# Mamba-2 layer and FFN on one core: decay blocks of 64 tokens instead of 128, with the order of the engines' work rewritten around them

## The chip, the cores and the metric

One core of one Trainium2 chip. The metric is device time in microseconds of one launch, as the median of 3 runs. Engines are called as in the profile: PE (TensorE matmul), PEld (its weight loads), DVE (VectorE), ACT (ScalarE), POOL (GpSimd), SP (SyncE, which issues DMAs).

## The reference

Input x is 8 batches of 512 tokens by 128, float32. Weights are inputs too.

```python
x = x + mamba(layernorm(x))          # 32 heads of 64 channels, 8 groups, state 64, conv width 4
x = x + ffn(layernorm(x))            # 128 -> 512 -> 128, ternary weights, gelu, two layernorms
# mamba: h = rmsnorm(u); z, xBC, dt_raw = split(h @ in_proj_w)
xBC = silu(causal_depthwise_conv4(xBC) + conv_b); xs, B, C = split(xBC)
dt = softplus(dt_raw + dt_bias); dA = exp(-exp(A_log) * dt)
for t in range(S):                   # per batch and head; B and C are shared by 4 heads
    h = dA[t] * h + (dt[t] * xs[t])[:, None] * B[t][None, :]
    y[t] = h @ C[t]
y = y + D * xs
g = y * silu(z)                      # then rms over each group of 256 channels
out = (g * rsqrt(mean(g**2) + eps) * gate_norm_w) @ out_proj_w
u + out
```

## The kernel before, in words

Names: P = 128, S = 512 tokens, NB = 8 batches, CH = 4 chunks of 128 tokens, UNITS = 4 (a unit is a pair of groups), R = 4, SLOTS = 16. The engines run five programs that meet only through semaphores (after, L354: wait until a counter has reached the value that belongs to batch b and index i).

**Slots.** A batch is 16 slots, n = 4q + r. Head pair m (one head of each group of unit q, 128 channels together) is worked on in several slots, a stage in each, as LAG_* says (L67): projection and convolution of its x tile in unit q; transposed x, decay scans, z projection in slot m+4 (SSD); masked decay matrix m+5 (M); states m+6 (STATE); y m+7 (Y); gating, squares, sums m+8 (SUM); variance m+12, norm factor m+13, normalising m+14, output projection m+15. Batch 0, and batches 7 and 8 (the drain) are unrolled; batches 1 to 6 are a hardware loop on every engine. In a slot each engine runs a fixed list that is written out by hand (functions slot). PLAN (L46) gives the projection tiles of a slot: one in r = 0 and 3, two in r = 1 and 2.

**The recurrence in chunks of 128.** For each head pair the kernel builds, for four chunks, a decay matrix L (128x128 for each of two heads) by a scan over the free dimension: the state starts from an identity matrix that lies in a PSUM bank and is multiplied by the decays spread over all partitions (DVE, two scans of 512, L1036). POOL multiplies it with C·B in one instruction of 1024 elements (L619). ACT makes xdt = dt*x out of the transposed x (8 instructions, L796) and xw = xdt times the last column of L (6 instructions, L755). PE makes three chunk states (L1384), DVE chains them (a copy L1059 and two steps L1062), and also makes cdec = C times the products of decays (L1070, from a copy of C in PSUM, L736). PE adds up y: within chunks (L1408) and from states (L1414). DVE adds D*x (skip, L1079); POOL multiplies by the gate (L605), ACT squares, POOL sums and, later, normalises (L611).

**Orders that matter.** PE in a slot: x transposes, projections (project, L1335; three matmuls each, of which the first waits until the bank, one of two that all tiles and z use in turn, is free), states, output projection (L1393), y complete, variance, bt transposes, z projection, C·B, factors, xn and xo transposes. The bank of z in r = 1 and 2 is that of the first tile of the same slot, free after its third tap (proj_free, L1317). All small transposes, states and C·B share two banks in turn (MISC, misc_plan, L92; misc_free, L1282). DVE: scans, taps (L1047, three per tile) with state steps between them, cdec, skip. ACT: copy of C, pend, xw, initial value of the convolution (L763), silu of the tiles of the slot before (L781), xdt, square, factors, bt copy, gate (L845), cbs copies (L852), rbs copy. POOL: gating, normalising, lm product, sum, power. SP: spread rows (L489: decays of two heads to all partitions, products to half the partitions each) for the slot four later, of which spread's ring has four places.

**Beginning.** LayerNorm and RMSNorm of the whole input, dt and decays (L965 to L1003, L715), then the decays are transposed in 8 row blocks (rows, L1270, L718), DVE makes running products for each chunk (L1013), SP stores both in DRAM (L483) and spreads them from there. Row blocks 1 to 7 are interleaved with slots 1 to 3 (EARLY_ROWS). **End.** A drain, ternary quantisation of the FFN weights beside it, and the FFN (ffn_steps), none of which the change touches beyond semaphore counts.

## Time and profile before

| | |
|---|---|
| median of 3 runs | 1308.03 us (1307.38 to 1315.56) |
| the profiled execution | 1308.41 us, span 1306.5 us, mean granted clock 0.924 |
| busy: PE, PEld, DVE, ACT, POOL | 1042.0 (80%), 718.9 (55%), 1099.3 (84%), 985.1 (75%), 863.5 (66%) |
| DMA | 127.10 MB, mean 97 GB/s |
| spread rows, DMA issues | decays 128 of 512 KB, products 256 of 128 KB |

The slots of batch 0 start near 77 us, head pairs are worked on from about 120 us, the loop over batches 1 to 6 ends near 1000 us, the drain near 1200, and the FFN fills the rest. A row of the timeline is start, length in us, engine, line, operation, tile written <- tiles read, shape, count, and in brackets the idle time of the engine before it with what ended it; equal instructions that follow each other are merged (x2), and then the length runs from the first start to the last end. Instructions overlap on an engine: the next one may start before the last has ended.

### The profile page before, as it was taken

To read this page: it belongs to the slowest core of one execution; us is meant where nothing else is said; L and a number is where in the kernel's file an instruction comes from. 1 tells how busy PE (TensorE), PEld (TensorE's weight loads), DVE (VectorE), ACT (ScalarE), POOL (GpSimd) and SP (SyncE) were. 2 spreads that over 40 slices of the span, in tenths; PEclk is the share of its full clock that TensorE was granted. 3 is DMA by queue.
4 is the path that set the end of the run, shared out by engine and by line. 5 is a ranking of instruction groups with operands and counts; after the bars stand their busy time and mean duration, and the time that the engine had idled before them with its cause. 6 is when DMAs were issued, how large, how long until landed. Compare 5 with 4: busy or idle time off the path is not lost. (4 is left out here: it accounts for less than half of the span.)

```text
span 1306.5 us, 29881 instructions
## 1 busy us (share of the span) xinstructions
PE 1042.0 (80%) x8556; PEld 718.9 (55%) x8556; DVE 1099.3 (84%) x1837; ACT 985.1 (75%) x2943; POOL 863.5 (66%) x584
## 2 busy tenths in 40 slices
PE   1423778888888888888888889979898888887786
PEld 1412555566555555665566566656566655653555
DVE  8756888889888888888888888888888999947995
ACT  3624778989788878888888888888888888862453
POOL 1540367877677868776777777776777888795321
PEclk9986789999899989998998998899988999998899
DMA  5532244534344334343443444443434344421301
GB/s 148 162 84 53 61 104 99 120 98 98 87 122 111 98 91 109 105 99 90 110 109 98 100 103 110 95 109 91 115 93 93 103 123 106 106 75 43 111 26 33
DMA packets 84864, 127.10 MB, mean 97 GB/s; under 512 B 18512, under 2 KB 29392, under 8 KB 84432
## 3 DMA queue, kind: packets, MB, share of 16 engines
q1 hardware_dynamic: 80464, 122.91, 37.4%
q10 hardware_dynamic: 4224, 2.10, 0.5%
q8 instruction: 79, 1.29, 0.4%
q14 instruction: 97, 0.79, 0.2%
HBM read 115.54 MB, written 9.44 MB: 96 GB/s over the span
## 5 line engine op out<-in xcount | busy, mean ns | idle before, releaser
L1047 DVE SCALAR_TENSOR_TENSOR conv<-bank,cw,conv 128x511 f32<-128x511 f32 (+2 forms) x576 | 412.0, 742 | 105.7 <-ACT conv L763 100.9
L619 POOL TENSOR_TENSOR lm<-lm,cbs 128x1024 f32<-128x1024 f32 x128 | 303.3, 2370 | 87.9 <-ACT xw L755 86.5
L1036 DVE TENSOR_TENSOR_SCAN lm<-spread,bank 128x512 f32<-128x512 f32 x256 | 297.5, 1203 | 16.5 <-issue 12.7
L796 ACT ACTIVATE xdt<-bank,dt_all 128x64 f32<-128x64 f32 x1024 | 221.0, 326 | 0.5 <-issue 0.5
L605 POOL TENSOR_TENSOR gated<-gated,gate 128x512 f32<-128x512 f32 x128 | 163.0, 1273 | 64.5 <-DVE gated L1079 62.7
L1347 PE MATMUL bank<-xn_hi,w_hi 128*128 (+1 forms) x320 | 161.1, 503 | 54.1 <-DVE conv L1047 54.1
L755 ACT ACTIVATE xw<-xdt,lm 128x64 f32<-128x64 f32 x768 | 196.2, 338 | 0.0
L625 POOL TENSOR_TENSOR ssum<-ssum,sq 128x512 f32<-128x512 f32 x96 | 123.5, 1287 | 109.8 <-ACT sq L810 107.5
L1408 PEld LDWEIGHTS bank<-lm,xdt 128*64 128x64 f32 x2048 | 112.6, 140 | 96.4 <-issue 95.6
L611 POOL TENSOR_TENSOR gated<-gated,rbs 128x512 f32<-128x512 f32 x128 | 164.1, 1283 | 1.5 <-ACT rbs L859 1.5
L763 ACT ACTIVATE conv<-bank,cb_bias,cw 128x512 f32<-128x512 f32 x192 | 142.2, 767 | 25.3 <-PE bank L1349 25.3
L1393 PE MATMUL bank<-gated,w_out 128*128 128x512 f32 x256 | 153.9, 685 | 2.7 <-POOL gated L611 2.7
L1408 PE MATMUL bank<-lm,xdt 128*64 128x128 f32 x2048 | 143.1, 283 | 0.0
L1349 PE MATMUL bank<-xn_hi,w_lo 128*128 (+1 forms) x320 | 136.6, 427 | 0.0
L1348 PE MATMUL bank<-xn_lo,w_hi 128*128 (+1 forms) x320 | 136.0, 425 | 0.0
L1369 PE MATMUL bank<-ident,chan 128*128 128x128 f32 x512 | 89.4, 303 | 49.6 <-ACT cbs L852 22.4
L845 ACT ACTIVATE gate<-bank 128x512 f32<-128x512 f32 x128 | 77.5, 605 | 58.3 <-PE bank L1349 57.3
L781 ACT ACTIVATE chan<-conv 128x512 f32<-128x512 f32 x192 | 112.9, 622 | 0.0
L1414 PE MATMUL bank<-cdec,hpk 64*64 64x128 f32 x1536 | 111.7, 278 | 0.0
L1079 DVE SCALAR_TENSOR_TENSOR gated<-chan,dskip,bank 128x512 f32<-128x512 f32 x128 | 94.9, 741 | 17.0 <-PE bank L1414 16.9
L1347 PEld LDWEIGHTS bank<-xn_hi,w_hi 128*128 128x128 f32 x320 | 66.2, 207 | 76.2 <-DVE conv L1047 66.3
L1369 PEld LDWEIGHTS bank<-ident,chan 128*128 128x128 f32 x512 | 64.1, 153 | 71.9 <-issue 36.5
(167 smaller groups left out, 1676.3 us busy)
## 6 DMA issues: line engine op xcount, KB each, us to landing
spread<-decay_scratch SPq DMA_DIRECT2D x128, 512.0 KB, 5.1
spread<-product_scratch SPq DMA_DIRECT2D x256, 128.0 KB, 5.6
lm<-in_L_attn_in_proj_w SPq DMA_DIRECT2D x1, 2048.0 KB, 9.9
xn_scratch<-chan SPq DMA_DIRECT2D x4, 512.0 KB, 5.4
r_stage<-residual_scratch SPq DMA_DIRECT2D x8, 256.0 KB, 2.8
x_scratch<-r_stage SPq DMA_DIRECT2D x8, 256.0 KB, 5.6
cbs<-x_scratch SPq DMA_DIRECT2D x8, 256.0 KB, 3.0
gated<-x_scratch SPq DMA_DIRECT2D x1, 2048.0 KB, 8.2
```

The lines of the kernel that those rows point to most:

```text
L605: gp.tensor_tensor(gated[:, v % 2, mr, :], gated[:, v % 2, mr, :], gate[:, mr, :], ALU.mult).then_inc(gated_done, 1)
L611: gp.tensor_tensor(gated[:, v % 2, m % R, :], gated[:, v % 2, m % R, :], rbs[:, :], ALU.mult).then_inc(normed, 1)
L619: gp.tensor_tensor(lm[:, mr, :, :], lm[:, mr, :, :], cbs[:, :, :], ALU.mult).then_inc(m_done, 1)
L755: act.activation(xw[:, mr % 2, c, half], xdt[:, mr, P * c + HP * a:P * c + HP * a + HP], ACT.Copy, scale=lm[:, mr, a, P * c + P - 1:P * c ...
L763: act.activation(conv[:, ci % 4, :], tile_bank(b, n, t)[:, :], ACT.Identity, scale=cw[:, q, t, KW - 1:KW], bias=cb_bias[:, q, t:t + 1]).th ...
L796: act.activation(xdt[:, r, at:at + HP], misc_of("xt", n)[:, at:at + HP], ACT.Copy, scale=dt_h).then_inc(xdt_done, 1)
L1036: V.tensor_tensor_scan(lm[:, m % R, a, :], spread[:, m % R, a, :], ident_bank[:, :], 0.0, ALU.mult, ALU.add).then_inc(scanned, 1)
L1047: V.scalar_tensor_tensor(out=conv[:, ci % 4, shift:S], in0=tile_bank(b, n, t)[:, 0:S - shift], scalar=cw[:, q, t, KW - 1 - shift:KW - shif ...
L1347: MM(out_b, wh, hi, start=True, stop=False)
L1369: last = TR(misc_of("xt", n)[:, P * c:P * c + P], chan[:, chan_of(mq, 2 + mr), P * c:P * c + P], ident)
L1393: last = MM(out_bank[:, :], w_out[:, m, :], gated[:, (m // R) % 2, m % R, :], start=(m == 0), stop=(m == SLOTS - 1))
L1408: MM(y_bank[half, tok], xdt[:, mr, P * c + HP * a:P * c + HP * a + HP], lm[:, mr, a, tok], start=(c == 0), stop=False)
```

## The change

1. Blocks of 64 tokens (NBLK = 8) take the place of chunks of 128. Partitions 0 to 63 hold the even blocks (e = 0) and 64 to 127 the odd ones. One scan of 512 elements makes L for both heads (2 heads x 4 blocks x 64), from a seed of repeated 64x64 identities. The lm product has 512 elements; lm has eight places instead of four.
2. Seven state steps (the first a copy) instead of three, from 14 state calls (64x64) instead of 6, in two groups (e = 0, 1). y takes 16 calls of 64x64x64 within blocks and 14 from states instead of 8 and 6. y lies in two banks (even and odd blocks), half a bank each, so skip is two instructions of 256.
3. xw is one DVE product of the transposed x, straight from PSUM, with wt_all (dt times decay to the block's end), which is made once at the beginning by PE products with masks (after_mask, upto_mask) and exponentials; the same gives the running products, so that DVE's scans there go. Rows of decays and products are transposed together and stored by three DMAs.
4. C product (cdec) and pend go to POOL, one slot later (slot m+5).
5. C·B, bt, rbs, xn and xo go to the spare halves of the two y banks; states and transposed x get a bank of their own; misc_plan and its turns go.
6. The orders change on all engines. PE: transposes and states first, interleaved and behind a wait for the state steps of the slot before, then projections, output projection, small transposes, y within blocks, z projection, y from states, variance. DVE: skip of the slot before (m+8 instead of m+7), scan, then state steps alternating with weight product and taps. ACT: silu ahead of the convolution's initial value, then xdt, square, then a wait for y, the spare-half copies (two of 256), gate, factors. POOL: lm product first, gating, pend and C product, normalising, sum.

The core of the diff:

```diff
@@ PE, slot
+                def states(e):
+                    bb, m = st
+                    rows_e = slice(BLK * e, BLK * e + BLK)
+                    for c in range(CH - e):
+                        for a in range(2):
+                            half = slice(HP * a, HP * a + HP)
+                            last = MM(s_bank[half, NS * (2 * c + e):NS * (2 * c + e) + NS], bt[rows_e, c, half],
+                                      xw[rows_e, m % R, P * c + HP * a:P * c + HP * a + HP], start=True, stop=True)
+                    last.then_inc(s_ready if e else s_low_done, 1)
...
+                if st is not None:
+                    bb, m = st
+                    after(pe, xw_done, SLOTS, bb, m)
+                    after(pe, bt_copied, 2 * UNITS, bb, 2 * (m // R) + 1)
+                    state_there(pe, bb, m - 1)
+                if ssd is not None:
...
+                    xdt_there(pe, bb, m - 1)
+                    if r == 1 and back(b, n - 1, LAG_VAR) is not None:
+                        vb, vm = back(b, n - 1, LAG_VAR)
+                        after(pe, var_copied, UNITS, vb, vm // R)
+                    x_transposes(0)
+                if st is not None:
+                    states(0)
+                if ssd is not None:
+                    x_transposes(1)
...
+                if st is not None:
+                    states(1)
+                if real:
+                    for t in PLAN[r]:
+                        project(b, n, t, (b, n))
...
+                    for c in range(CH):
+                        for e in range(2):
+                            rows_e = slice(BLK * e, BLK * e + BLK)
+                            for a in range(2):
...
+                                last = MM(y_bank[e][half, BLK * c:BLK * c + BLK], xdt[rows_e, mr, P * c + HP * a:P * c + HP * a + HP],
+                                          lm[rows_e, m % (2 * R), at:at + BLK], start=(c == 0), stop=False)
+                    last.then_inc(y_intra_done, 1)
+                if ssd is not None:
+                    project(b, n, "z", ssd)
+                if yy is not None:
...
+                    for k in range(1, NBLK):
...
+                            last = MM(y_bank[e][half, BLK * c:BLK * c + BLK], hpk[half, m % 2, k - 1, :],
+                                      cdec[half, m % R, BLK * k:BLK * k + BLK], start=False, stop=(k >= NBLK - 2))
+                    last.then_inc(y_ready, 1)
@@ DVE, slot
+                def skip():
+                    bb, m = yy
+                    v, mr = divmod(m, R)
+                    after(dve, y_ready, SLOTS, bb, m)
+                    if (m + LAG_Y) % R == 0 and back(b, n, 1 + LAG_SSD) is not None:
+                        cbb, cm = back(b, n, 1 + LAG_SSD)
+                        after(dve, cb_copied, 2 * UNITS, cbb, 2 * (cm // R) + 1)
...
+                if yy is not None:
+                    skip()
+                if ssd is not None:
+                    scan()
+                work_list = []
+                if ssd is not None:
+                    work_list.append((weigh, ()))
+                if real:
+                    work_list += [(one_tap, (shift, t)) for shift in range(1, KW) for t in PLAN[r]]
+                for k in range(max(NBLK - 1, len(work_list))):
+                    if state is not None and k < NBLK - 1:
+                        state_step(k)
+                    if k < len(work_list):
+                        work_list[k][0](*work_list[k][1])
@@ POOL, slot
+                    gp.tensor_copy(pend[:, mr, :].unsqueeze(2),
+                                   spread[:, mr, 1, :].rearrange("p (k i) -> p k i", i=BLK)[:, :, BLK - 1:BLK]).then_inc(pend_done, 1)
+                    after(gp, silu_done, NCONV, bb, CONV_ORDER.index((v, 1)))
+                    after(gp, y_ready, SLOTS, bb, m - R)
+                    gp.tensor_tensor(cdec[:, mr, :], spread[:, mr, 1, :], chan[:, chan_of(v, 1), :], ALU.mult).then_inc(cdec_done, 1)
@@ ACT, slot
+                if back(b, n, LAG_Y) is not None:
+                    bb, m = back(b, n, LAG_Y)
+                    after(act, y_ready, SLOTS, bb, m)
+                if r == 0 and ssd is not None:
...
+                    for a in range(2):
+                        act.activation(cbs[:, v % 2, S // 2 * a:S // 2 * a + S // 2], spare(a), ACT.Copy).then_inc(cb_copied, 1)
@@ PE, beginning
+            for first, mask in ((2, upto_mask), (6, after_mask)):
+                for k in range(2):
+                    MM(bank[first + k][:, :], mask, steps[:, S * k:S * k + S], start=True, stop=True).then_inc(cum_ready, 1)
```

## Rows read from the trace of the kernel before

**Rows 1.** Windows: us, busy (count) of each engine, PEclk, DMA share, GB/s

```profile
545.00:678.00 133.00, 115.79 (x991) 78.77 (x989) 115.00 (x185) 111.74 (x351) 98.84 (x65) 0.92 0.41 102
1075.00:1106.00 31.00, 27.45 (x251) 18.48 (x251) 28.62 (x47) 27.72 (x88) 24.98 (x17) 1.00 0.46 103
```

**Rows 2.** Timeline of DVE, one unit of four slots behind the loop

```profile
1074.65 0.74 DVE L1079 SCALAR_TENSOR_TENSOR gated<-chan,dskip,bank 128x512 f32<-128x512 f32 x1
...
1080.97 0.74 DVE L1079 SCALAR_TENSOR_TENSOR gated<-chan,dskip,bank 128x512 f32<-128x512 f32 x1
...
1086.12 1.42 DVE L1047 SCALAR_TENSOR_TENSOR conv<-bank,cw,conv 128x511 f32<-128x511 f32 x2 [2.10 <-ACT conv L763]
...
1091.18 0.74 DVE L1079 SCALAR_TENSOR_TENSOR gated<-chan,dskip,bank 128x512 f32<-128x512 f32 x1
...
1099.37 0.74 DVE L1079 SCALAR_TENSOR_TENSOR gated<-chan,dskip,bank 128x512 f32<-128x512 f32 x1
1100.03 2.32 DVE L1036 TENSOR_TENSOR_SCAN lm<-spread,bank 128x512 f32<-128x512 f32 x2
1102.27 1.50 DVE L1047 SCALAR_TENSOR_TENSOR conv<-bank,cw,conv 128x511 f32<-128x511 f32 x2
...
1103.83 0.73 DVE L1047 SCALAR_TENSOR_TENSOR conv<-bank,cw,conv 128x509 f32<-128x509 f32 x1
1104.48 0.58 DVE L1062 SCALAR_TENSOR_TENSOR hpk<-hpk,pend,bank 128x64 f32<-128x64 f32 x2
1104.98 0.68 DVE L1070 TENSOR_TENSOR cdec<-spread,bank 128x512 f32<-128x512 f32 x1
1105.58 0.74 DVE L1079 SCALAR_TENSOR_TENSOR gated<-chan,dskip,bank 128x512 f32<-128x512 f32 x1
```

**Rows 3.** Waits: waiting engine and line <- releaser: us in total, times, longest

```profile
DVE conv L1047 <- ACT conv L763: 100.9, 64, 4.7
```

**Rows 4.** Timeline of PE, slots r = 2 and r = 3 of that unit

```profile
1093.22 0.57 PE L1384 MATMUL bank<-xw,bt 128*64 128x64 f32 x12
...
1094.78 1.09 PE L1408 MATMUL bank<-lm,xdt 128*64 128x128 f32 x16
...
1098.07 0.50 PE L1347 MATMUL bank<-xn_hi,w_hi 128*128 128x512 f32 x1 [1.39 <-DVE conv L1047]
...
1098.63 0.39 PE L1349 MATMUL bank<-xn_hi,w_lo 128*128 128x512 f32 x1
1098.86 0.60 PE L1369 MATMUL bank<-ident,chan 128*128 128x128 f32 x4
...
1102.66 0.87 PE L1414 MATMUL bank<-cdec,hpk 64*64 64x128 f32 x12
1103.47 0.50 PE L1347 MATMUL bank<-xn_hi,w_hi 128*128 128x512 f32 x1
```

**Rows 5.** Timeline of PE and DVE behind the edge of the loop

```profile
612.80 1.11 PE L1369 MATMUL bank<-ident,chan 128*128 128x128 f32 x4 [3.23 <-issue]
...
613.95 2.33 DVE L1036 TENSOR_TENSOR_SCAN lm<-spread,bank 128x512 f32<-128x512 f32 x2 [2.68 <-issue]
```

**Rows 6.** Groups: out<-in, shapes, count | busy us, mean ns | idle before, releaser

```profile
L619 POOL TENSOR_TENSOR lm<-lm,cbs 128x1024 f32<-128x1024 f32 x128 | 303.3, 2370 | 87.9 <-ACT xw L755 86.5
L605 POOL TENSOR_TENSOR gated<-gated,gate 128x512 f32<-128x512 f32 x128 | 163.0, 1273 | 64.5 <-DVE gated L1079 62.7 <-ACT gate L845 1.2 <-issue 0.2
...
L1013 DVE TENSOR_TENSOR_SCAN sq<-ssum,bt 32x128 f32<-32x128 f32 x16 | 6.1, 431 | 5.1 <-ACT ssum L723 5.1
```

**Rows 7.** Timeline of ACT, two places in that unit and behind it

```profile
1099.06 0.60 ACT L845 ACTIVATE gate<-bank 128x512 f32<-128x512 f32 x1 [0.94 <-PE bank L1349]
...
1113.77 1.09 ACT L852 ACTIVATE cbs<-bank 128x512 f32<-128x512 f32 x2 [0.49 <-PE bank L1446]
```

**Rows 8.** Timeline of ACT at the beginning, row blocks

```profile
104.54 0.59 ACT L723 ACTIVATE ssum<-bank 32x512 f32<-32x512 f32 x1 [17.84 <-DMA product_scratch<-rbs]
```

**Rows 9.** DMA issues: line, count, KB each, median us to landing

```profile
spread<-decay_scratch SPq DMA_DIRECT2D x128, 512.0 KB, 5.1
```

More of the change, by code:

```diff
@@ L427, in build, with blocks, spare, xo_half @@
         NSMALL = 2 + 2 * UNITS * 4 + 4 + 4
-        def misc_position(kind, n, k=0):
-            return [j for j, x in enumerate(MISC) if x[0] == n and x[1] == kind][k]
-        def misc_of(kind, n, k=0):
-            return misc_bank[misc_position(kind, n, k) % 2][:, :]
+        def blocks(t):
+            return t.rearrange("p (c e s) -> p c e s", e=2, s=BLK)
+        def spare(e):
+            return y_bank[e][:, S // 2:S]
+        def xo_half(b, e):
+            return bank[4][:, S // 2 * e:S // 2 * e + S // 2] if isinstance(b, int) and b == NB else spare(e)
         block = ctx.enter_context(nc.Block())
@@ new lines, in skip @@
+                    if (m + LAG_Y) % R == 2 and back(b, n, 1 + LAG_NORM) is not None:
+                        cbb, cm = back(b, n, 1 + LAG_NORM)
+                        after(dve, rbc_copied, 2 * UNITS, cbb, 2 * (cm // R) + 1)
+                    for e in range(2):
+                        V.scalar_tensor_tensor(out=blocks(gated[:, v % 2, mr, :])[:, :, e, :],
+                                               in0=blocks(chan[:, chan_of(v, 2 + mr), :])[:, :, e, :],
+                                               scalar=dskip[:, m:m + 1],
+                                               in1=y_bank[e][:, 0:S // 2].rearrange("p (c s) -> p c s", s=BLK),
+                                               op0=ALU.mult, op1=ALU.add).then_inc(skipped, 1)
@@ new lines, in one_tap @@
+                def one_tap(shift, t):
+                    ci = CONV_ORDER.index((q, t))
+                    if shift == 1:
+                        after(dve, acc_init, NCONV, b, ci)
+                    else:
+                        after(dve, tap, NTAP, b, TAP[q, t, shift - 1])
+                    V.scalar_tensor_tensor(out=conv[:, ci % 4, shift:S], in0=tile_bank(b, n, t)[:, 0:S - shift],
+                                           scalar=cw[:, q, t, KW - 1 - shift:KW - shift],
+                                           in1=conv[:, ci % 4, shift:S], op0=ALU.mult, op1=ALU.add).then_inc(tap, 1)
@@ L1188, in _ @@
             for n in range(SLOTS):
-                for i in EARLY_ROWS.get(n, ()):
-                    rows(i)
+                if n == 2:
+                    dve.wait_ge(dtstep_a, 7)
+                    V.tensor_tensor(wt_all[:, :, :], wt_all[:, :, :], dt_all[:, :, :], ALU.mult).then_inc(wt_ready, 1)
                 slot(0, n)
@@ new lines, in slot @@
+                if r == 1 and back(b, n, LAG_M) is not None:
+                    if isinstance(b, int) and b == 0:
+                        after(pe, cb_copied, 2 * UNITS, b, 2 * (n // R) - 1)
+                    for c in range(CH):
+                        last = TR(spare(c // 2)[:, P * (c % 2):P * (c % 2) + P], chan[:, 0, P * c:P * c + P], ident)
+                    last.then_inc(bt_ready, 1)
+                if r == 2 and back(b, n, LAG_NORM) is not None:
+                    bb, m = back(b, n, LAG_NORM)
+                    after(pe, rexp_done, UNITS, bb, m // R)
+                    for c in range(CH):
+                        last = TR(spare(c // 2)[:, P * (c % 2):P * (c % 2) + P], rexp[:, 2 * c:2 * c + 2, :].rearrange("p a d -> p (a d)"), ident)
+                    last.then_inc(rbc_ready, 1)
@@ new lines, in slot @@
+                if n == XN_SLOT and following(b) is not None:
+                    pe.wait_ge(staged, b * 16 + 16)
+                    for c in range(CH):
+                        last = TR(spare(c // 2)[:, P * (c % 2):P * (c % 2) + P], xn_stage[:, c, :], ident)
+                    last.then_inc(xnt_ready, 1)
+                if n == XO_SLOT and back(b, n, SLOTS) is not None:
+                    bb, _ = back(b, n, SLOTS)
+                    after(pe, out_copied, 1, bb, 0)
+                    for c in range(CH):
+                        last = TR(xo_half(b, c // 2)[:, P * (c % 2):P * (c % 2) + P], ocm[:, P * c:P * c + P], ident)
+                    last.then_inc(xo_ready, 1)
@@ L1463, in slot @@
-                if n == XO_SLOT and back(b, n, SLOTS) is not None:
-                    bb, _ = back(b, n, SLOTS)
-                    after(pe, out_copied, 1, bb, 0)
-                    misc_free(b, n, "xo")
-                    for c in range(CH):
-                        last = TR(misc_of("xo", n)[:, P * c:P * c + P], ocm[:, P * c:P * c + P], ident)
-                    last.then_inc(xo_ready, 1)
             def step(i, par, k):
```

588 lines of the change are left out of this document (250 added, 338 removed).

## The prediction

> **What bounds the kernel now.** I read the windows by stage first [rows 1]. A turn of the loop over batches takes 133 us with PE and DVE busy 115 to 116, ACT 112, POOL 99: no engine alone explains it. Behind the loop there is a clean stretch of 31 us (clock 1.00, DVE busy 28.6), one unit of four slots (r = 0 to 3; two tiles are convolved in r = 1 and 2, one in r = 0 and 3), and everything below is worked out on it. The skip instruction (L1079) closes a slot on DVE: it starts at 1074.65, 1080.97, 1091.18, 1099.37 and 1105.58 [rows 2], so the slots take 6.3, 10.2, 8.2 and 6.2 us, the unit 30.9. DVE works without a pause except ahead of the taps of r = 1, where 2.1 us end with ACT's L763; such waits cost 100.9 us over the run [rows 3]. So DVE bounds the kernel, with one wait a unit. PE does not: in r = 2 it stands 1.39 us until a DVE tap has freed a projection bank [rows 4], and nobody waits for this, because y's matmuls (L1408, L1414) come ahead of that z projection. A turn costs 133 and not four times 30.9, since at its edge DVE and PE stand 2.7 and 3.2 us for nothing that the profile shows, and then PE's transposes take 1.11 instead of 0.60 us: the granted clock is at its lower level there, and 0.92 in the mean of the turn [rows 1, 4, 5].
>
> **DVE's own work.** Distances from start to next start [rows 2]: scan 1.12 (two in 1100.03 to 1102.27), tap 0.65, skip 0.66, C product 0.60, two chained state steps 0.50, so 0.31 for a step that the next one waits for and 0.19 for one with other work behind it; the copy is taken as a step. Before: 8 scans 9.0, 18 taps 11.7, 4 skips 2.6, 4 C products 2.4, 12 steps 2.3: 28.0 us. After: 4 scans 4.5; 18 taps 11.7; 28 steps 5.3, and 0.5 for those that chain at the end of r = 0 and 3; 8 half skips: the line through 0.19 for 64 elements and 0.66 for 512 gives 0.39 for 256 (bounds 0.33 and 0.66), 3.1; 4 weight products from PSUM with a repeated operand: nearest row the C product, 0.60 (lower bound half of it, upper a scan, 1.12), 2.4. Sum 27.5: DVE alone gains 0.5 us a unit, 15 us of the run. (About 1%, 13 us, is what a measurement can tell from no change.) The four scans and the C product that leave are eaten by sixteen state steps, weight products and split skips.
>
> **ACT, POOL, SP.** ACT loses six weight copies and the pend copy a slot, about 1.5 us; that would end DVE's 2.1 us wait if nothing else came. POOL's lm product halves from 2.37 to about 1.27, and a C product of 512 elements costs 1.27 by L605 (bounds 0.60, DVE's time for it, and 2.37) [rows 6]; with a small pend copy it is even, and POOL has 34 of 133 us free. On SP one more DMA issue a slot for decays is hidden: scans use rows requested over two slots earlier, and the volume falls.
>
> **PE gets many small matmuls.** Six state calls of 64 columns (12 instructions) start within 0.57-0.22 = 0.35 us, 0.058 a call; eight calls of 128 columns within 1.09-0.27 = 0.82, 0.11 a call [rows 4]. After: 14 state calls 0.81, y inside blocks 16 calls 0.93, y from states 14 calls 0.80 (was 0.60), and in r = 0 C with B 16 calls 0.93. From one tile shape to another costs 0.2 (last L1414 starts 1102.66+0.60, L1347 at 1103.47); a slot has about four more of these. Bounds for each 16-call group: half of it (rival C) and 1.7, at today's 0.11 a call.
>
> **The order is what costs.** (1) y's last matmuls now stand behind the z projection, and in r = 1 and 2 z still waits for the third tap of the slot's first tile. (2) The skip of that y opens DVE's next slot, with scan and taps queued behind it; after slots r = 0, 1, 2 it also waits until ACT, which waits for y itself, has copied the two spare halves. (3) PE opens a slot with transposes and states that wait for DVE's last state step of the slot before (in r = 2 also for ACT's bt copies, in r = 1 for var's copy), and behind them stand the projections on which L763 and the taps wait. So DVE, PE and ACT form one ring per slot, where today three chains run side by side.
>
> Let X be the end of that third tap in r = 1. z: first matmul at 0.06, last 0.56 later [rows 4], 0.62; then 0.43 (its 512 columns 0.23 and a shape change), y's first state matmul 1.05, last 1.85; y there at 2.16 (0.27 length, 0.04 signal). ACT's two half copies: 0.49 apart for 512 elements (1.09-0.60 [rows 7]), 0.26 to 0.4 for 256: done 2.85. DVE: skip halves 2.87 to 3.65, scan to 4.77. PE starts the next slot at 2.89, after bt. Two transposes, 8 state calls, two transposes with a wait in their midst, 6 state calls, three shape changes: last start 1.69 on; the projection's last start 2.46, and ACT starts 0.43 after it (1098.63 to 1099.06 [rows 4, 7]): 2.90. ACT conv 5.8 to 6.6, first tap 6.62. Four taps and four steps (3.4) and the last tap's own 0.74: X' = 10.75. Slot r = 2 takes 10.75 against 8.2 before.
> r = 3, from X': y there 2.16, copies 2.85, scan to 4.77; PE needs no bt, starts 2.05, projection there 4.95, first tap 5.78, three taps and seven steps to 9.03. PE behind its projection: out 1.06 (1.56 from states to y [rows 4] less 0.50), y inside, z, y from states with changes: y there 9.07. Both meet.
> r = 0: skip 9.09, transposes 9.1, first tap 12.8, last step 16.1; PE with C and B (0.93 and a change), y inside, z, y one behind another: y there 17.1, ACT's copies 17.8, skip of r = 1 at 17.8.
> r = 1: PE waits for var's copy (8 matmuls, 0.9 behind y; ACT behind its gate): 18.5; projection 21.4, first tap 22.2, X again at 26.35.
> Unit 10.75+26.35 = 37.1 against 30.9: 6.2 more.
>
> At this point a rule bears on the sum. The rows show the two column halves side by side: 12 instructions of 0.22 us within 0.57 us. The Trainium skill, "TensorE: Matmul & The Clock Gate", section "Part 3: Packing small matmuls", says that matmuls on different row and column tiles run at the same time. By it the 16-call groups, which now touch all four quarters of the array, take half of 0.93; by the pace of the rows all of it. Nothing here shows which; it is rival C.
>
> **Sum.** 31 units (32 less one for slots without work at the beginning): 192. Clock: 0.92 means about 21 of 133 us at the lower level; PE's matmuls had slack there and are then over half of the ring: 2 to 8 us a turn, I take 4, six turns, 24. Beginning: ACT stands 17.84 us until row stores get through behind the spread loads of four slots [rows 8]; these have 512+2x128 KB each [rows 9] and get 512, a third less, -5.5; DVE's four product scans a batch (1.4 to 1.5 by L1013 [rows 6]) leave the chain of row blocks, -7 over five of them; four mask products and a seed product, at the lower clock 1 us an instruction of 512 columns (out's two take 1.06 at the upper one), about +5: -8 (bounds -14 and +5). FFN: 0. The profiled execution took 1308.41 (span 1306.5 and what lies around it), almost the median of the runs, 1308.03. 1308.4+192+24-8 = 1516; forecast 1515.
>
> **Rivals.** A, DVE decides, faster: 0.5 of its work and the 2.1 us wait go: 31x2.6 = 81, with -8: 1219. For it: DVE is the bound today. It decides if z and y take under 0.85 us from X (a step and a tap are left on DVE then), and z alone takes 0.6. 5%. B, the ring closes at today's length, 31 us: 1300; 4%. C, four quarters side by side: 0.46 less in r = 3, 0.93 in r = 0 (hidden in r = 1, 2): 1.4x31 = 43, so 1472; 15%. D, half of my waits overlap (shape changes free, shorter copies), unit 34: 1308+96+12-8 = 1408; 14%. The forecast, 1480 to 1590, 62%. Range 1400 to 1590: the cases above reach it with C and D, the long side by half skips of 0.66 and weight products of 1.12 on the ring. Faster 0.05, same 0.04, slower 0.91.
>
> **What would show it.** Right: skips wait for y or for ACT's copies after r = 0, 1 and 2; first taps wait for L763 in every slot; DVE's busy share in a turn falls from 0.86 to about 0.75 with busy time of a unit near 28.5; a turn of 160 us. Wrong: a turn under 145 us, DVE busy over 0.85, z not waiting for taps, or 16-call groups in 0.5 us.

## The result, and the profile after

The changed kernel takes 1500.54 us (median of 4 runs, 1494.83 to 1507.69), the kernel before 1307.76 in the runs beside it: a ratio of 1.146, 95% interval 1.140 to 1.153. The forecast was 1515, its range 1400 to 1590. The profiled execution has a span of 1499.5 us, 193.0 more than before.

The windows of the changed kernel, the stage in the loop and a stretch of one unit behind it (the columns are those of [rows 1]), and two lines of its page, the sums by engine and the granted clock in 40 slices:

```profile
545.00:705.00 160.00, 132.68 (x1859) 93.30 (x1853) 116.22 (x255) 85.89 (x243) 103.11 (x96) 0.88 0.22 62
1256.00:1292.00 36.00, 29.43 (x445) 21.57 (x437) 26.38 (x59) 19.19 (x54) 23.88 (x24) 0.91 0.23 60
```

```profile
PE 1160.9 (77%) x15222; PEld 827.5 (55%) x15222; DVE 1088.2 (73%) x2325; ACT 778.5 (52%) x2090; POOL 893.6 (60%) x848
...
PEclk9986699989898998898999889898999999996899
```

In 160 us of the loop DVE is busy 116.2, a share of 0.73 where it had 0.86 [rows 1], and the mean granted clock is 0.88 for 0.92. The clock line shows that the lower level is met all through the loop, and the clean stretch has only 0.91, where the kernel before had 1.00.

DVE's timeline of one unit, from the skip that opens r = 2 on (the counterpart of [rows 2]):

```profile
1260.93 0.87 DVE L1030 SCALAR_TENSOR_TENSOR gated<-chan,dskip,bank 128x256 f32<-128x256 f32 x2 [1.95 <-ACT bt L823]
1261.72 1.22 DVE L1044 TENSOR_TENSOR_SCAN lm<-spread,bank 128x512 f32<-128x512 f32 x1
...
1264.59 0.75 DVE L1068 SCALAR_TENSOR_TENSOR conv<-bank,cw,conv 128x511 f32<-128x511 f32 x1 [0.63 <-ACT conv L777]
...
1272.88 0.87 DVE L1030 SCALAR_TENSOR_TENSOR gated<-chan,dskip,bank 128x256 f32<-128x256 f32 x2 [3.31 <-ACT rbs L831]
...
1278.88 0.87 DVE L1030 SCALAR_TENSOR_TENSOR gated<-chan,dskip,bank 128x256 f32<-128x256 f32 x2
...
1282.83 0.75 DVE L1068 SCALAR_TENSOR_TENSOR conv<-bank,cw,conv 128x511 f32<-128x511 f32 x1 [0.63 <-ACT conv L777]
...
1286.61 0.87 DVE L1030 SCALAR_TENSOR_TENSOR gated<-chan,dskip,bank 128x256 f32<-128x256 f32 x2 [0.51 <-ACT cbs L816]
```

The skip (L1030) opens a slot. It waits for ACT's copies after r = 1 (1.95 us), r = 2 (3.31) and r = 0 (0.51), and not after r = 3. The slots take 11.95 us (r = 2), 6.00 (r = 3) and 7.73 (r = 0); the r = 1 slot ahead of them, from 1248.69, takes 12.24. The unit is 37.9 us; 30.9 was before, 37.1 the forecast.

PE's timeline of slots r = 2 and r = 3 of this unit (the counterpart of [rows 4]):

```profile
1265.65 0.69 PE L1459 MATMUL bank<-lm,xdt 64*64 64x64 f32 x32
1268.78 0.79 PE L1321 MATMUL bank<-xn_hi,w_hi 128*128 128x512 f32 x1 [2.43 <-DVE conv L1068]
1269.37 0.63 PE L1322 MATMUL bank<-xn_lo,w_hi 128*128 128x512 f32 x1
1269.80 0.63 PE L1325 MATMUL bank<-xn_hi,w_lo 128*128 128x512 f32 x1
1270.36 1.71 PE L1473 MATMUL bank<-cdec,hpk 64*64 64x64 f32 x28
...
1275.62 0.69 PE L1459 MATMUL bank<-lm,xdt 64*64 64x64 f32 x32
1276.24 0.50 PE L1321 MATMUL bank<-xn_hi,w_hi 128*128 128x512 f32 x1
...
1277.13 1.03 PE L1473 MATMUL bank<-cdec,hpk 64*64 64x64 f32 x28
```

In r = 2 PE is done with y inside the blocks at 1266.3 and stands 2.43 us for the tap. What comes behind the stand is at the lower of the two clock levels (1.2 GHz): z's matmuls take 0.63 us where they take 0.40 at the upper one (2.4 GHz) in r = 3, and y's 28 from the states 1.71 where they take 1.03. In the kernel before z waited for the same tap, but y stood ahead of it: ACT's gate waited for z (0.94 us in [rows 7]), the skip didn't.

Not every such stand has the lower level behind it. PE's timeline of the slot r = 1 before this one, and of r = 2 three units earlier:

```profile
1252.09 0.63 PE L1325 MATMUL bank<-xn_hi,w_lo 128*128 128x512 f32 x1
...
1258.20 0.50 PE L1321 MATMUL bank<-xn_hi,w_hi 128*128 128x512 f32 x1 [1.80 <-DVE conv L1068]
...
1259.09 1.03 PE L1473 MATMUL bank<-cdec,hpk 64*64 64x64 f32 x28
```

```profile
1157.54 0.50 PE L1321 MATMUL bank<-xn_hi,w_hi 128*128 x1 [2.43 <-DVE conv L1068]
...
1158.44 1.03 PE L1473 MATMUL bank<-cdec,hpk 64*64 64x64 f32 x28
```

Of 60 waits of z in the timeline of the whole run, 16 have z and y behind them at the lower level and 6 a part of y; of the 25 waits of 2.43 or 2.44 us it is 9 and 4. The first row shows a second place: the projections at the opening of r = 1, behind the eight variance matmuls and a wait of 0.51 us for ACT, are at the lower level in 21 of 30 units.

The waits of the changed kernel (as in [rows 3]), of the groups POOL's two products (as in [rows 6]), and one DMA line (as in [rows 9]):

```profile
PE bank L1321 <- DVE conv L1068: 138.7, 62, 4.2
...
DVE conv L1068 <- ACT conv L777: 103.4, 125, 11.3
...
DVE gated L1030 <- ACT bt L823: 71.0, 31, 3.4
DVE gated L1030 <- ACT rbs L831: 69.5, 30, 3.4
...
DVE gated L1030 <- ACT cbs L816: 18.2, 23, 2.1
```

```profile
L610 POOL TENSOR_TENSOR lm<-lm,cbs 128x512 f32<-128x512 f32 x128 | 163.8, 1280 | 50.8 <-ACT cbs L816 38.5
...
L627 POOL TENSOR_TENSOR cdec<-spread,chan 128x512 f32<-128x512 f32 x128 | 164.0, 1281 | 0.0
...
spread<-decay_scratch SPq DMA_DIRECT2D x256, 128.0 KB, 3.3
```

z's wait comes twice a unit (62 times), and DVE's new waits at the skip sum to 159 us. The convolution's wait is the same in sum but twice as frequent (64 times before).

Where the 193 us lie: the first skip starts at 145.5 us (153.1 before), the last at 1366.2 (1176.7 before), and behind it come 133.3 us (129.8 before). So the beginning gives 7.6, the slots cost 197.1, and the end 3.5.

### The profile page after: what moved, and what is told of

It is laid out like the page before. It is cut to its first block and busy times, and to the rows that moved or that the text cites. A ratio compares the mean times of both kernels' runs of the same rounds, so it can differ in the third digit from the quotient of the medians.

```text
span 1499.5 us, 43588 instructions
## 1 busy us (share of the span) xinstructions
PE 1160.9 (77%) x15222; PEld 827.5 (55%) x15222; DVE 1088.2 (73%) x2325; ACT 778.5 (52%) x2090; POOL 893.6 (60%) x848
## 5 line engine op out<-in xcount | busy, mean ns | idle before, releaser
L1068 DVE SCALAR_TENSOR_TENSOR conv<-bank,cw,conv 128x511 f32<-128x511 f32 (+2 forms) x576 | 427.4, 744 | 104.0 <-ACT conv L777 103.4
L1321 PE MATMUL bank<-xn_hi,w_hi 128*128 (+1 forms) x320 | 173.7, 543 | 138.7 <-DVE conv L1068 138.7
L1030 DVE SCALAR_TENSOR_TENSOR gated<-chan,dskip,bank 128x256 f32<-128x256 f32 x256 | 111.5, 477 | 176.9 <-ACT bt L823 71.0
L617 POOL TENSOR_TENSOR gated<-gated,gate 128x512 f32<-128x512 f32 x128 | 164.0, 1281 | 100.2 <-DVE gated L1030 100.0
L1082 DVE SCALAR_TENSOR_TENSOR hpk<-hpk,pend,bank 128x64 f32<-128x64 f32 x768 | 210.1, 274 | 5.5
L610 POOL TENSOR_TENSOR lm<-lm,cbs 128x512 f32<-128x512 f32 x128 | 163.8, 1280 | 50.8 <-ACT cbs L816 38.5
L1367 PE MATMUL bank<-ident_t,chan 128*128 128x128 f32 x512 | 122.9, 325 | 89.2 <-issue 26.2
L1346 PE MATMUL bank<-xw,bt 64*64 64x64 f32 x3584 | 173.2, 238 | 0.0
L627 POOL TENSOR_TENSOR cdec<-spread,chan 128x512 f32<-128x512 f32 x128 | 164.0, 1281 | 0.0
L1346 PEld LDWEIGHTS bank<-xw,bt 64*64 64x64 f32 x3584 | 136.1, 145 | 44.3 <-issue 31.1
L1321 PEld LDWEIGHTS bank<-xn_hi,w_hi 128*128 128x128 f32 x320 | 68.0, 213 | 166.9 <-DVE conv L1068 147.9
L1473 PEld LDWEIGHTS bank<-cdec,hpk 64*64 64x64 f32 x3584 | 127.6, 147 | 51.4 <-issue 50.8
L1044 DVE TENSOR_TENSOR_SCAN lm<-spread,bank 128x512 f32<-128x512 f32 x128 | 155.3, 1213 | 0.0
L1325 PE MATMUL bank<-xn_hi,w_lo 128*128 (+1 forms) x320 | 147.5, 461 | 0.0
L1473 PE MATMUL bank<-cdec,hpk 64*64 64x64 f32 x3584 | 146.2, 236 | 0.2
```

The source lines that it names most:

```text
L610: gp.tensor_tensor(lm[:, at, :], lm[:, at, :], cbs[:, v % 2, :], ALU.mult).then_inc(m_done, 1)
L617: gp.tensor_tensor(gated[:, v % 2, mr, :], gated[:, v % 2, mr, :], gate[:, mr, :], ALU.mult).then_inc(gated_done, 1)
L627: gp.tensor_tensor(cdec[:, mr, :], spread[:, mr, 1, :], chan[:, chan_of(v, 1), :], ALU.mult).then_inc(cdec_done, 1)
L1068: V.scalar_tensor_tensor(out=conv[:, ci % 4, shift:S], in0=tile_bank(b, n, t)[:, 0:S - shift], scalar=cw[:, q, t, KW - 1 - shift:KW - shif ...
L1082: V.scalar_tensor_tensor(out=hpk[:, m % 2, k, :], in0=hpk[:, m % 2, k - 1, :], scalar=pend[:, m % R, k:k + 1], in1=s_bank[:, NS * k:NS * k ...
L1321: MM(out_b, wh, hi, start=True, stop=False)
```

## The experiments

All are compared with the kernel before in runs beside them; a difference from the changed kernel is taken from its 1500.5 us. The line numbers are those of each kernel.

### Where the ring closes: y ahead of z, and the taps tile by tile

```diff
-                if ssd is not None:
-                    project(b, n, "z", ssd)
                 if yy is not None:
...
                     last.then_inc(y_ready, 1)
+                if ssd is not None:
+                    project(b, n, "z", ssd)
```

y's two groups write the same banks from different row halves of the array, and the kernel has a wait between them, in the changed kernel on z's third matmul; here out's matmul was cut into two column halves, and the second carries it.

> Edit: y's matmuls from the states stand ahead of the z projection again, as in the kernel before; the wait for y's matmuls inside the blocks, which z's third matmul carried, is carried by the second half of out's matmul, which is cut in two for it. Nothing else moves. Ring theory (a slot is DVE to PE to ACT to DVE, with z in the middle of it in r = 1 and 2): y comes about 2.4 us earlier in r = 1 and 2, in which PE stands for a tap, and 0.6 us earlier in r = 0 and 3; some of it is met by the next thing that is late (DVE's own 28 us a unit), so a unit falls from 37.5 to about 33, and the time to 1345, between 1310 and 1400. PE's stand of 2.4 us in the two slots is then behind y, and harms nobody. Rival (the amount of small matmuls on PE is what costs, not their order): no change, 1480 to 1510.

Measured: 1347.24 us, ratio 1.030 (1.027 to 1.034). This one move gives back 153 of the 193 us, where the ring had said 1345, and the amount of small matmuls is the same, so the rival falls. The mean granted clock of the profiled run rises with it, from 0.891 to 0.939, which the expectation hadn't priced: the 153 us are the order and the clock together.

```diff
-                    work_list += [(one_tap, (shift, t)) for shift in range(1, KW) for t in PLAN[r]]
+                    work_list += [(one_tap, (shift, t)) for t in PLAN[r] for shift in range(1, KW)]
```

The table of tap numbers is changed in the same way.

> Edit: DVE's six taps of a slot with two tiles go tile by tile and no longer shift by shift. The last tap of the first tile, for which z waits, comes two taps and two steps earlier, some 1.9 us; the last tap of the second tile stays where it was. Ring theory: z and y come back up to 1.9 us earlier in r = 1 and 2, the two slots with two tiles; a unit falls by 2 to 3.8 us, the time to between 1385 and 1440, PE's stand ahead of z shrinks from 2.4 to about 0.5 us, and the granted clock rises over 0.89. Chained taps of one tile follow one another at once now; that may cost some 0.1 us each of the twelve (two steps fill most gaps), 1.2 a unit at most. Rival (z's wait is not on the ring, y is late from PE's work): no change or slower by the chained taps, 1495 to 1540.

Measured: 1362.23 us, ratio 1.041 (1.036 to 1.046). It gives back 138 us, 23 more than the best of the expectation. The windows of both kernels, first y ahead of z, then tile by tile:

```profile
545.00:705.00 160.00, 144.19 (x2194) 109.07 (x2194) 135.08 (x297) 101.95 (x286) 123.50 (x116) 0.96 0.25 68
```

```profile
545.00:705.00 160.00, 142.89 (x2119) 101.88 (x2119) 132.38 (x292) 97.90 (x278) 118.20 (x110) 0.93 0.23 67
```

Not only is the tap earlier: the clock in the loop goes from 0.88 to 0.93. The expectation had the clock rise, but priced the time alone. PE's timeline of tile by tile shows the z projection of a slot r = 2: it waits 0.73 us for its tap, not 2.43, and runs at the upper level behind it:

```profile
1133.50 0.50 PE L1321 MATMUL bank<-xn_hi,w_hi 128*128 128x512 f32 x1 [0.73 <-DVE conv L1068]
```

### What the clock costs: more matmuls in the stand

```diff
+                    if r in (1, 2):
+                        after(pe, xw_done, SLOTS, *ssd)
+                        xdt_there(pe, *ssd)
+                        for k in range(5):
+                            MM(xt_bank[:, :], w_hi[:, ssd[1] // R, CONVS + r, :], xn_of(xn_hi, ssd[0]), start=True, stop=True)
                     project(b, n, "z", ssd)
```

> Edit, on the changed kernel: in r = 1 and 2 PE gets five more matmuls of 512 columns between y's matmuls inside the blocks and the z projection, into the bank of the transposed tiles after all its readers are done; their result is used nowhere. So PE has more work and the place where it stood for 2.4 us is filled; the order is otherwise the same. Clock theory (the granted clock falls to its lower level after a stand of this length, and matmuls of the ring then take 0.63 instead of 0.40 us and 0.054 instead of 0.030 an instruction): the mean granted clock of a turn rises from 0.88 to 0.93 or more, r = 1 and 2 lose 0.7 to 1.5 us each, the time falls to between 1400 and 1470 though there is more work. Rival (the clock's level has nothing to do with this stand, or costs nothing on the ring): z comes later by what the five matmuls outlast the stand, up to 0.8 us a slot; no change or slower, 1495 to 1550.

Measured: 1458.87 us, ratio 1.117 (1.115 to 1.120): 42 us faster, with 10 more matmuls a unit. The window in the loop, and PE's timeline in r = 1:

```profile
545.00:705.00 160.00, 140.80 (x1970) 99.67 (x1968) 120.92 (x266) 90.28 (x258) 104.13 (x97) 0.95 0.23 65
```

```profile
1210.80 1.40 PE L1467 MATMUL bank<-xn_hi,w_hi 128*128 128x512 f32 x5
1212.40 0.50 PE L1321 MATMUL bank<-xn_hi,w_hi 128*128 128x512 f32 x1 [0.20 <-DVE conv L1068]
...
1213.29 1.03 PE L1478 MATMUL bank<-cdec,hpk 64*64 64x64 f32 x28
```

The five matmuls fill the stand to within 0.20 us, z and y behind it run at the upper level (y 1.03 for 1.71 us), and the clock of the stage is 0.95. Of 57 waits of z in this run, none over 0.43 us, not one has z at the lower level behind it (22 of 60, in whole or in part, in the changed kernel). So the long stands bring the lower level, though not each of them, and it is worth about 42 us, more if what is left counts too: the opening of r = 1 is still at the lower level in 15 of 29 units. The DVE tap comes as late as before, and in r = 2 the added matmuls themselves start 0.68 us late, behind a wait for ACT (a row not shown).

### Quarters of the array

```diff
-                    for c in range(CH):
-                        for e in range(2):
+                    for e in range(2):
+                        for c in range(CH):
```

> Edit: the 16 matmuls of y inside the blocks are issued with the block's half e outermost, so that eight calls in a row touch only two quarters of PE's array, where the changed kernel touches all four in turn. Nothing else moves. The profile of the changed kernel has these groups within 0.65 to 0.71 us by its own records and some 0.42 us of starts. If the four quarters working side by side are what makes them that short, the group goes to the 0.93 us of the forecast's term, 0.5 us more in r = 3 and r = 0, where it is on the ring, and nothing in r = 1 and 2, where PE stands for a tap anyway: 31 to 40 us more, 1525 to 1540. Rival (a small matmul is simply short, whatever quarter it is in): no change within 5 us.

Measured: 1518.71 us, ratio 1.161 (1.155 to 1.168), 18 more. The group of r = 3 in this run:

```profile
1284.66 0.98 PE L1459 MATMUL bank<-lm,xdt 64*64 64x64 f32 x32
1285.57 0.50 PE L1321 MATMUL bank<-xn_hi,w_hi 128*128 128x512 f32 x1
```

Less some 0.21 us for the length of the last one, the 31 distances take 0.77 us here and 0.48 in the changed kernel (0.69 at 1275.62): 24.8 ns an instruction for two quarters, 15.5 for four. A loss of 0.29 us in r = 3 and r = 0 is 0.58 a unit, times 31 is 18 us, what was measured. So the order of the calls sets the pace, and the rival falls. One thing isn't parted by this run: with e outermost eight calls in a row also stay in one of y's two banks, where they alternated. The expectation took 0.5 us for each group, and even two quarters come in 0.77 and not in 0.93. By the Trainium skill, "TensorE: Matmul & The Clock Gate", section "Part 3: Packing small matmuls", matmuls in different tiles of the array run at the same time. Here the trace agrees in so far as the order over four quarters is the faster one, by these two numbers.

### Is DVE's own line on the ring

```diff
-                if yy is not None:
-                    skip()
                 if ssd is not None:
                     scan()
+                if yy is not None:
+                    skip()
```

> Edit: on DVE the decay scan of a slot stands ahead of the skip and no longer behind it. The scan waits for nothing of this slot, so its 1.2 us fill the time in which the skip waits for y and for ACT's copies. Ring theory: the taps behind skip and scan wait for ACT's convolution in nearly every slot, so the scan was hidden already, and the slot is set by PE and ACT: no change to speak of, 1470 to 1505 (a gain of up to 1 us a unit in the slots where the state step behind the scan comes earlier). Rival (DVE's own line of skip, scan and weight product is what the slot waits for once y is there): 1.2 us in each of three slots whose skip waits, 3.6 a unit, 1390.

Measured: 1512.15 us, ratio 1.156 (1.149 to 1.163): no gain, rather 12 more, and 7 above the range of the expectation. The scan does not bind, as the ring says; DVE's line as the bound falls. DVE's timeline:

```profile
1274.48 1.21 DVE L1044 TENSOR_TENSOR_SCAN lm<-spread,bank 128x512 f32<-128x512 f32 x1
1276.51 0.87 DVE L1030 SCALAR_TENSOR_TENSOR gated<-chan,dskip,bank 128x256 f32<-128x256 f32 x2 [0.83 <-ACT rbs L831]
...
1279.32 0.75 DVE L1068 SCALAR_TENSOR_TENSOR conv<-bank,cw,conv 128x511 f32<-128x511 f32 x1 [0.63 <-ACT conv L777]
```

In this slot z and y ran at the upper level, and the skip's wait is 0.83 us; in the changed kernel it is 1.94 in such slots (at 1122.29, say), and 3.31 at 1272.88, where they ran at the lower one. The time did not follow. Over the run the skip's waits for bt and rbs fall from 141 to 65 us, while DVE's wait ahead of the state copy grows from 49 to 114 and the first taps' for ACT from 103 to 117: what the scan fills at the skip, DVE stands again behind it.

```diff
+                if state is not None and ssd is not None:
+                    state_step(0)
+                    work_list[0][0](*work_list[0][1])
+                    work_list = [None, None, None] + work_list[1:]
```

with the loop behind it starting at step 1 and passing over None: the order on DVE is copy, weight product, steps 2 to 4, first tap.

> Edit, on the changed kernel as it is: the state steps two to four ahead of the first tap, nothing else. Ring theory: the first taps' wait for ACT's convolution (103 us in 125 waits) takes them in, and fewer steps stand between the taps that PE's z waits for: 0.4 to 0.6 us a slot, 1.5 to 2.5 a unit, and 1500 falls to between 1420 and 1455. Rival (with z waiting for a tap the slots are set elsewhere, and moving 0.2 us steps is nothing): 1490 to 1505.

Measured: 1476.9 us, ratio 1.130 (1.122 to 1.139), 24 less. It lies between both expectations. The first taps' wait for ACT halves, from 103.4 us in 125 waits to 49.5 in 61, so it does take in the steps, but z's stand for the tap remains (PE bank L1325 <- DVE conv: 129.5 us in the waits of this run, 138.7 in the changed kernel).

### A miss: projections ahead of transposes and states

```diff
+                if real:
+                    for t in PLAN[r]:
+                        project(b, n, t, (b, n))
                 if st is not None:
                     bb, m = st
                     after(pe, xw_done, SLOTS, bb, m)
```

(and gone from behind the states.)

> Edit, on the changed kernel: PE issues a slot's projections ahead of the transposes and the state matmuls, with the waits for DVE's last step and for ACT's copies behind them. Ring theory: ACT's convolution, for which the first tap waits in every slot, no longer has 1.7 to 2.2 us of transposes and states in front of it, and in r = 2 and 1 it is past the copies of bt and var too; against it DVE's first step and weight product come 0.6 to 1.2 us later. Per unit 3 to 6 us less: 1330 to 1420. Rival (DVE's state steps and the weight product, fed by the transposes and states, are what the first taps are queued behind, so that the gain of the one is the loss of the other): 1470 to 1500.

Measured: 1569.1 us, ratio 1.201 (1.199 to 1.203): slower than either said. Part of that is the clock's: the stand ahead of z grows (PE bank L1321 <- DVE conv: 215.3 us in 67 waits, 138.7 in 62 in the changed kernel), 40 of 63 such waits have z at the lower level behind them, and the mean granted clock is 0.855. With y ahead of z as well:

> Edit: y ahead of z, and the projections ahead of transposes and states. In the run with y ahead r = 1 takes 10.6 us, of which DVE stands 3.0: 1.34 ahead of the first state step and 1.66 ahead of the first taps, both behind PE's wait for var's copy; the first taps of the other slots wait 0.63 each. Ring theory: the convolution is past these, r = 1 falls by 1.5 to 2 us, the others by 0.6 at most, if the states come no later than DVE needs them: 1347 less 31 x 2 to 3.5, 1240 to 1285, less than the kernel before. Rival (the state steps then come later by the time of the projections, 0.7 us in r = 0 and 3 and 1.4 in r = 1 and 2, and the taps are queued behind them): 1330 to 1370.

Measured: 1397.38 us, ratio 1.067 (1.064 to 1.071), 50 more than without it, and above its rival's 1370 too. DVE's timeline of the first of the two:

```profile
1291.72 0.87 DVE L1030 SCALAR_TENSOR_TENSOR gated<-chan,dskip,bank 128x256 f32<-128x256 f32 x2 [3.35 <-ACT rbs L831]
1292.51 1.21 DVE L1044 TENSOR_TENSOR_SCAN lm<-spread,bank 128x512 f32<-128x512 f32 x1
1295.88 0.23 DVE L1079 COPY hpk<-bank 128x64 f32<-128x64 f32 x1 [2.15 <-issue]
...
1296.81 0.74 DVE L1068 SCALAR_TENSOR_TENSOR conv<-bank,cw,conv 128x511 f32<-128x511 f32 x1
```

The first tap no longer waits for ACT, but it is queued behind the state copy, and this stands 2.15 us. The profile names no releaser for it; by PE's timeline the states, which PE now issues last, end 0.45 us ahead of the copy (1294.52 and 0.91 long). The wait has changed its name and grown. That the queue order carries it is read from these rows; a version with the taps ahead of the copy, which would show it, wasn't run. So the 0.6 us at the first tap were not a gain to be had on PE's side.

### Is there a version that beats both

> Edit: y ahead of z and the taps tile by tile, both at once. Each alone took over 130 us off the changed kernel. Ring theory: both cut the same wait (z's, for the tap), so they don't add up: with y ahead, z delays only the next slot's transposes and states, PE's stand of 1.11 us in r = 2 and 0.66 in r = 1 goes, and some 1 us a unit comes off 1347: 1310 to 1335. Rival (they are two costs): 1347 less another 100: 1210 to 1260. If the chained taps cost more than the stand: 1347 to 1360.

Measured: 1319.69 us, ratio 1.010 (1.008 to 1.012). The two edits cut the same wait and don't add up, as the ring said.

On top of it, the steps in the wait (the DVE edit above):

> Edit, on the version with y ahead of z and the taps tile by tile: on DVE the second, third and fourth state step of a slot stand right behind the weight product, ahead of the first tap, and no longer one behind each tap. In that version DVE still stands 93 us in 122 waits of the first taps for ACT's convolution, some 0.6 us a slot, and a slot of r = 0 or 3 ends with three chained steps in 0.9 us. Ring theory: two steps chained, 2 x 0.31, fill that wait, and the chained end goes: 0.6 us less in r = 0 and 3, 0.2 to 0.4 in r = 1 and 2, 1 to 2 us a unit, 1320 to between 1260 and 1290, less than before. Rival (PE, busy 147 of 160 us, is the bound by now and DVE's waits are only its shadow): 1310 to 1320.

Measured: 1301.96 us, ratio 0.995 (0.993 to 0.997): 18 us less, a little over half of the least expected. Then also the variance ahead of z:

```diff
+                if r == 0 and back(b, n, LAG_VAR) is not None:
...
                 if ssd is not None:
                     project(b, n, "z", ssd)
-                if r == 0 and back(b, n, LAG_VAR) is not None:
```

(on ACT the copy vtok moves ahead of the gate in the same way.)

> Edit: the one of the run beside this, and PE's eight matmuls of the variance stand ahead of the z projection in r = 0, with ACT's copy of them ahead of its gate. PE waits for that copy at the opening of r = 1 (0.45 us in the run with y ahead of z), and DVE's first state step there 1.3 us for the states behind it. Ring theory: the opening of r = 1 comes 0.4 to 0.8 us earlier, 12 to 25 us less than the run beside this. Rival (r = 1 is set by the projection banks or PE's own work, z being 0.9 us later): no difference, within 5 us.

Measured: 1265.13 us, ratio 0.966 (0.962 to 0.970), 37 us less than the run beside it, more than expected. The windows of the two, and of the second the start of a slot r = 1 on DVE:

```profile
545.00:705.00 160.00, 149.22 (x2260) 111.64 (x2259) 140.88 (x308) 106.92 (x297) 126.46 (x120) 0.95 0.26 71
```

```profile
545.00:705.00 160.00, 150.14 (x2370) 113.43 (x2365) 146.52 (x321) 112.06 (x308) 132.27 (x123) 0.99 0.28 74
```

```profile
1059.78 0.87 DVE L1030 SCALAR_TENSOR_TENSOR gated<-chan,dskip,bank 128x256 f32<-128x256 f32 x2 [0.60 <-ACT cbs L816]
1060.56 1.21 DVE L1044 TENSOR_TENSOR_SCAN lm<-spread,bank 128x512 f32<-128x512 f32 x1
1062.59 0.23 DVE L1079 COPY hpk<-bank 128x64 f32<-128x64 f32 x1 [0.81 <-issue]
```

The clock is 0.99 in the loop for 0.95: PE's wait for ACT at the opening of r = 1 (0.45 us in the run with y ahead of z) is gone, and z's three large matmuls now stand between the eight small ones of the variance and the next slot. The projections of r = 1 were at the lower level in 12 of 29 units of the run beside it and are in none of 29 here. The clock's share came on top of the 12 to 25 us of the expectation. A turn takes 126.4 us, from skip to skip, against 133 before, and DVE is busy 0.92 of it. This is the fastest version measured: the change with its order put right is 3.4% faster than the kernel before. No run makes the same moves on the kernel before, so it isn't shown how much of this the blocks of 64 give and how much the order.

> Edit: the fastest version so far (y ahead of z, tile by tile, steps in the wait, variance ahead of z: 1265 us) with the decay scan ahead of the skip on DVE. In it DVE stands 0.60 us ahead of the skip of r = 1 and 0.81 ahead of the first state step behind the scan. Ring theory: the scan fills the first, but the skip, on which y's next matmuls wait, comes 1.2 us later where DVE did not stand; PE has these 1.2 us of slack only in some slots (it is busy 150 of 160 us): between 15 us less and 15 us more, 1250 to 1280. Rival (DVE alone sets the slot by now, busy 146.5 of 160 us): 31 x 0.6 less, 1246.

Measured: 1280.07 us, ratio 0.977 (0.971 to 0.983), 15 more than without. DVE stands elsewhere for what it fills, and the skip comes 1.2 us later for POOL's gate product, whose wait for it goes up from 29.6 to 73.8 us.

## Why the prediction was right, and where its terms were off

**The ring.** Right, in place and in size. y ahead of z alone gave back 153 us; the skips wait after r = 0, 1 and 2 and not after r = 3, as step (2) says. Forecast and measured slots: r = 1 11.4 and 12.2, r = 2 10.75 and 11.95, r = 3 6.2 and 6.0, r = 0 8.7 and 7.7. Where no lower level falls into the slot, it fits better still: r = 1 takes 11.3 us (from 664.05 and from 903.01) and r = 2 10.84 (from 718.74). "First taps wait for L763 in every slot" holds in three slots of the unit shown, not in r = 3: there ACT's convolution is done when DVE comes to the tap, behind a skip that waited 3.31 us and also behind one that waited 1.94 (at 1122.29).

**From X on.** X, the end of the third tap, is 1268.74 in r = 2. The forecast has the next skip at X+2.87; it came at X+4.14. The way from the skip that opens r = 2 to this X held: it was to take 10.75-2.87 = 7.88 us and took 1268.74-1260.93 = 7.81. So the whole miss of r = 2 is the 1.27 us in z and y, which run at the lower level (z's last matmul starts 0.44 us later than forecast, counted from X, y's first another 0.13, and y is there another 0.64 later).

**The clock: mis-sized and misplaced.** The forecast put 24 us on the edges of the loop's turns and took the upper level inside a unit, as [rows 4] had it. The stands ahead of z, which the forecast itself had found, bring the lower level behind 22 of 60, and the opening of r = 1 is at it in 21 of 30 units. The run with extra matmuls prices what it takes away at 42 us. The stand of 1.39 us before [rows 4] had left z at its 0.50 us, and this was taken to hold for a longer one. A reading of the kernel before was short here too: the prediction put all of the 9 us between a turn and four clean units on the loop's edge, but slots r = 1 inside the loop took up to 12.4 us where the clean one takes 10.2, with PE at the lower level:

```profile
690.70 0.63 PE L1348 MATMUL bank<-xn_lo,w_hi 128*128 x1
```

In the turn around this row, 686.19 to 819.19, the four slots r = 1 make 4.9 of the 9 us.

**The 16-call groups: mis-sized.** Forecast 0.93 us, measured 0.48. The prediction itself lists "16-call groups in 0.5 us" among the signs of being wrong: this sign came, and none of the others. Rival C's mechanism fits, though not its result. The row that the prediction read as two column halves side by side (12 instructions of 0.22 us within 0.57) doesn't show that by itself: four transposes over the whole array, 0.27 us each, lie within 0.60 in [rows 4] as well, so lengths overlap without any halves. One group in r = 3 and two in r = 0 on the ring, 0.45 each, are 42 us less. Slots r = 0 and 3 are 1.2 us shorter than forecast, nearly that.

**The sum.** The forecast had 192 for the slots and 24 for the clock, 216. With the groups as measured and the clock at the 42 us of the extra matmuls it is 192-42+42 = 192; measured 197. The same comes from the slots: those without the lower level add up to 11.3+10.84+6.0+7.7 = 35.8 us a unit, nearly the forecast's 37.1 less the 1.35 of the groups, and 31 x (35.8-30.9) = 152 leaves 45 for the clock. The ring was right, but that the total came within 1% is partly luck: with the groups right and the clock as forecast it would have been about 1474, with the clock right and the groups as forecast about 1534. The beginning gave 7.6 of 8 us, the end cost 3.5 of 0. POOL's C product, with 1281 ns, is the 1.27 forecast.

**DVE's own work.** Forecast 27.5 us a unit. In the stretch of 36 us it is busy 26.4, which makes 27.8 for the unit's 37.9, and in the fastest version slots r = 2 and 3, where DVE never pauses, take 8.2 and 6.0. DVE's share in the loop was to fall to 0.75 and fell to 0.73; the turn was to be 160 us and is 158.4 (933.4 to 1091.8, skip to skip).

**Rivals.** A, DVE as the bound, falls with the waits at the skip, and scan_first shows that DVE's line had slack. B, a ring of today's length (31 us), falls with the unit's 37.9, and D (waits overlap, unit of 34) with it. No rival named the clock inside the unit.

## What to carry to other kernels

When a change puts the matmuls that others wait for behind one that waits for a late buffer, look for the loop this closes through the engines, and move the awaited matmuls ahead of the waiting one first: that was 153 of 193 us. The 153 hold the clock's share too. A stand of TensorE can cost twice, once as time and once as clock for what follows: stands of about 2 us and more did here in part of the cases, so work out the forecast with the work behind a new one at either level. A test of a ring is to shorten one arm (it must pay) and to fill a wait on another arm (it must not).

## What the runs showed of the hardware

In the changed kernel 16 of 60 waits of z, of 1.7 to 3.6 us, were followed by z at the lower clock level; behind waits of 2.43 us both levels are met. With five extra matmuls in them 57 waits of 0.20 to 0.43 us were left, all followed by the upper level, and the kernel was 42 us faster. In the run with y ahead of z 57 waits of z were of up to 1.2 us, all followed by the upper level; stands of 0.66 and 1.11 us were followed by matmuls of 0.50 us, the upper level:

```profile
1147.25 0.50 PE L1321 MATMUL bank<-xn_hi,w_hi 128*128 128x512 f32 x1 [0.66 <-DVE conv L1068]
...
1155.87 0.50 PE L1321 MATMUL bank<-xn_hi,w_hi 128*128 128x512 f32 x1 [1.11 <-DVE conv L1068]
```

The length of the stand isn't all of it: in the same run the wait of 0.45 us at the opening of r = 1, with eight matmuls of two columns ahead of it, has the lower level behind it:

```profile
1138.28 0.41 PE L1370 MATMUL bank<-ident_t,chan 128*128 128x128 f32 x2 [0.45 <-ACT vtok L860]
...
1140.72 0.63 PE L1322 MATMUL bank<-xn_lo,w_hi 128*128 128x512 f32 x1
```

64x64 matmuls of 64 columns start 15.5 ns apart when they go round all four quarters of the array, 24.8 ns when eight calls in a row keep to one row half and both column halves, and 30 ns (1.03 us for 28, less the last one's 0.21) where they alternate between two quarters on the diagonal, all at the upper level. But the states' first group (16 instructions within 0.68 us), also one row half and both column halves, comes at 31 ns. Why the groups over two quarters differ no run here tells.
